# Self products over type-sorted nodes, a pass without branches, and one comparison for six row one-hots in a graph kernel

## The reference

```python
h = relu(layernorm(x))
xr = einsum('nd,rde->rne', h, W_rel)                       # 3 products
agg = segment_sum(xr[edge_type, src] + b_rel[edge_type], dst)
xs = einsum('nd,tde->tne', h, W_self)                      # 3 products
h_self = xs[node_type, arange(N)] + b_self[node_type]      # each node keeps one of them
x = x + relu(h_self + agg)
# layer 1: q, k, v from relu(layernorm(x)); softmax over the in-edges of each node; output product
```

## Time and profile before

| | us |
|---|---|
| runs of the kernel, median (lowest to highest) | 350.64 (350.07 to 350.78) |
| the profiled execution, its own time | 351.21 |
| its span, from the first to the last instruction | 349.4 |

### The profile page before, as it was taken

How to read it: one execution, slowest core, us unless ns; L and a number is a source line. 1 busy time by engine, 2 the same in 40 slices (tenths; PEclk the granted TensorE clock), 3 DMA queues, 4 the chain that set the end, 5 groups by cost and what they waited for, 6 DMA issues and landing times.

```text
span 349.4 us, 5835 instructions
## 1 busy us (share of the span) xinstructions
PE 310.5 (89%) x2113; PEld 247.3 (71%) x2113; DVE 213.7 (61%) x546; ACT 143.0 (41%) x276; POOL 70.0 (20%) x92
## 2 busy tenths in 40 slices
PE   3527449998999999999989999999899999999994
PEld 2104326766777777886878878999788888888883
DVE  5685994789994333343343695387685647574721
ACT  1009311151311333225234254367786655564621
POOL 4002350063250320337000141041000101010101
PEclk9999686999999999999999999999999999999999
DMA  5702311003021030000361000000000000000000
GB/s 166 240 1 60 123 63 58 2 1 120 3 83 40 3 122 2 2 3 2 120 190 52 1 0 2 0 2 0 1 3 2 2 30 2 32 2 32 2 32 27
DMA packets 7324, 14.19 MB, mean 41 GB/s; under 512 B 630, under 2 KB 646, under 8 KB 7290
## 3 DMA queue, kind: packets, MB, share of 16 engines
q1 hardware_dynamic: 6836, 13.13, 11.1%
q10 hardware_dynamic: 454, 0.61, 0.6%
HBM read 12.46 MB, written 1.28 MB: 39 GB/s over the span
## 4 chain that ended last, share of the span: by engine, by line
PE 74%; DVE 14%; ACT 4%; issue 3%; DMA 2%; DVEq 1%; POOL 0%; ACTq 0%
PE banks L1135 23%; PE banks L1081 8%; PE banks L1121 8%; PE banks L1215 7%; PE banks L1201 6%; PE banks L1190 6%; PE banks L1235 4%; PE banks L990 4%; DVE key_hot L725 3%; DVE row_hot L724 3%; DMA raw<-in_L_gnn_W_qkv_dram 2%; PE banks L1225 1%; PE banks L1111 1%; PE banks L1098 1%; PE banks L1067 1%
## 5 line engine op out<-in xcount | busy, mean ns | idle before, releaser
L389 POOL TENSOR_TENSOR w_hl<-raw,w_hl 128x512 fp32r<-128x512 f32 x24 | 30.6, 1298 | 88.4 <-ACT w_hl L457 88.4
L1135 PE MATMUL banks<-w_hl,hT 128*128 128x512 f32 x180 | 48.0, 418 | 0.0
L913 DVE CUSTOM_DVE_ANT_0 s_sb<-banks,mask_add 128x640 f32<-128x640 f32 x40 | 32.6, 821 | 22.1 <-PE banks L1190 22.0
L725 DVE TENSOR_SCALAR key_hot<-iota,picked 128x480 f16<-128x480 f16 x100 | 41.6, 416 | 0.0
L1135 PEld LDWEIGHTS banks<-w_hl,hT 128*128 128x128 f32 x180 | 35.2, 202 | 8.5 <-issue 0.2
L990 PE MATMUL banks<-key_hot,row_hot 128*128 128x480 f16 x100 | 28.4, 421 | 14.2 <-DVEq L755 14.0
L596 ACT ACTIVATE p_sb<-s_sb,neg_max 128x640 f32<-128x640 f32 x40 | 32.9, 823 | 17.3 <-DVE neg_max L913 17.3
L724 DVE TENSOR_SCALAR row_hot<-iota,picked 128x128 f16<-128x128 f16 x100 | 33.0, 330 | 6.5 <-issue 4.8
L1081 PE MATMUL banks<-adjT,h 128*128 128x320 f16 x240 | 33.8, 299 | 0.4 <-DVE zT_even L790 0.4
L466 ACT ACTIVATE adjT<-banks 128x480 f16<-128x480 f32 x20 | 11.3, 566 | 53.0 <-PE banks L1013 53.0
L1081 PEld LDWEIGHTS banks<-adjT,h 128*128 128x128 f16 x240 | 23.0, 98 | 10.5 <-issue 1.0
(11 more groups left out here) (160 smaller groups left out, 481.2 us busy)
## 6 DMA issues: line engine op xcount, KB each, us to landing
raw<-in_L_gnn_W_self_dram SPq DMA_DIRECT2D x3, 1024.0 KB, 5.8
raw<-in_L_gnn_W_rel_dram SPq DMA_DIRECT2D x3, 1024.0 KB, 5.2
raw<-in_L_gnn_W_qkv_dram SPq DMA_DIRECT2D x3, 1024.0 KB, 5.3
xs<-in_x_dram SPq DMA_DIRECT2D x1, 1024.0 KB
raw<-in_L_gnn_W_ff_dram SPq DMA_DIRECT2D x1, 1024.0 KB, 5.5
out_dram<-ybuf SPq DMA_DIRECT2D x4, 256.0 KB, 2.0
bv_rows<-in_L_gnn_b_qkv_dram ACTq DMA_DIRECT2D x1, 256.0 KB
bff_rows<-in_L_gnn_b_ff_dram ACTq DMA_DIRECT2D x1, 256.0 KB
```

Source lines behind the costliest of these rows:

```text
L389: nc.gpsimd.tensor_tensor(w_hl[q % 2][:, 1, kt], raw[q % 2][:, kt], w_hl[q % 2][:, 0, kt].bitcast(F32), ALU.subtract).then_inc(s_wlo, 1)
L725: return nc.vector.tensor_scalar(to_key, iota[:], float(KEYS * w), key, ALU.add, ALU.is_equal)
L913: nc.vector.tensor_tensor_reduce(s_sb[:, n % NS, :].rearrange("p (a j) -> p a j", a=2), banks[:, c:c + 2, 0:HALF], mask_add[:, it, :].rear ...
L1135: ins = mm(to, lhs[:, pl, kt, it * P:(it + 1) * P], weights[:, pw, kt, c0:c0 + cn], start=(start and n == 0), stop=(n == 3 * KD - 1), skip ...
```

## The change

1. **Self products over sorted nodes.** After the layer norm, the rows of `h` go to DRAM in the order of their type (each type starts at a multiple of 128), by five indirect scatters that POOL issues, one per tile, into a buffer that ACT's queue has first filled with zeros (1.8 MB). SP reads it back as 7 tiles (`hs`). PE transposes each tile (4 transposes) and multiplies it with its own type's weights only, as plain 32-bit floats: 4 matmuls of 512 columns, with the weights' place taken from a register. ACT copies both results out of PSUM. SP writes the 7 products to DRAM, and POOL gathers them back with five indirect transfers to `self_sum`. The 15 `self` units, the `hT` units, the split of `W_self` and the masking on DVE go. The positions come from ranks: one matmul with a triangle and five with ones on PE, and seven small chained instructions on DVE (`sorted_places`).
2. **No branches in the pass.** `G` is 6, so the loop for further chunks, the remainder and their register loads leave the windows. If a window had more than 6 chunks, all windows of the half would be counted again (`all_groups`, `all_chunks`), behind one branch for each half.
3. **One comparison for six row one-hots.** `row_hot` for a window is one `tensor_tensor` of two 16-bit tensors with 768 outputs a partition, one of them read with a step of 0 in the innermost dimension; the key one-hots stay as they are.
4. **Order.** The statistics come before window 1 on DVE. The pieces of the self products are `pipe`: two transposes and a product after window 6, then mostly one transpose and one product after each of windows 7 to 12. The relation weights 0 and 1 are split after the last of them.

```diff
-    G, F = 5, 3
+    G, F = 6, 1
+    PIPE_AT, PIPE_STEP = 6, 1
+    SORTED = NT + T - 1
...
-        side[2] = [("hT", 0, 0), ("hT", 1, 0)]
-        for it in range(2, NT):
-            side[it + 1].append(("hT", it, 0))
-        for n in range(T * NT):
-            side[5 + n].append(("self", n // NT, n % NT))
...
+        pipe = [("turn", 0), ("turn", 1)]
+        for t in range(SORTED):
+            pipe += [("self", t)] + [("turn", t + 2)] * (t + 2 < SORTED)
+        for n, u in enumerate(pipe):
+            pipe_side[PIPE_AT + max(n - 1, 0) * PIPE_STEP // 2].append(u)
...
+            self_weights(0)
+            sp.wait_ge(s_scat, 16 * NT)
+            for half, (t0, t1) in enumerate(((0, 2), (2, SORTED))):
+                sp.dma_start(hs[:, t0:t1, :], sorted_d[t0 * P:t1 * P, :].rearrange("(t p) d -> p t d", p=P)
+                             ).then_inc(s_hs[half], 16)
+            self_weights(1)
+            self_weights(2)
+            for q in range(R + 4):
+                if q == 2:
+                    for t in range(SORTED):
+                        sp.wait_ge(s_pcopy, pipe_no[("self", t)] + 1)
+                        sp.dma_start(self_d[t * P:(t + 1) * P, :], hs[:, t, :]).then_inc(s_kept, 16)
...
+            pool.wait_ge(s_place, 1)
+            pool.wait_ge(s_zero, 16)
+            for it in range(NT):
+                pool.wait_ge(s_y0, it + 1)
+                nc.gpsimd.indirect_dma_start(sorted_d, bass.IndirectOffsetOnAxis(ap=place_u[:, it:it + 1], axis=0),
+                                             in0[:, it, :], None).then_inc(s_scat, 16)
+            for it in range(NT):
+                pool.wait_ge(s_h16hi, it + 1)
+                nc.gpsimd.tensor_tensor(h16[:, 1, it, :], in0[:, it, :], h16[:, 0, it, :], ALU.subtract
+                                        ).then_inc(s_h16lo, 1)
             for kt in range(KD):
-                weights_lo(4, kt)
+                weights_lo(0, kt)
+            pool.wait_ge(s_kept, 16 * SORTED)
+            for it in range(NT):
+                nc.gpsimd.indirect_dma_start(self_sum[:, it, :], None, self_d,
+                                             bass.IndirectOffsetOnAxis(ap=place_u[:, it:it + 1], axis=0)
+                                             ).then_inc(s_self, 16)
+            for kt in range(KD):
+                weights_lo(1, kt)
...
+                nc.vector.tensor_tensor(row_hot[:, par], iota[:, 0:P].unsqueeze(1).broadcast_to([P, G, P]),
+                                        picked_row[:, w * G:(w + 1) * G].unsqueeze(2).broadcast_to([P, G, P]),
+                                        ALU.is_equal)
                 for k in range(G):
                     n = w * G + k
-                    one_hots(row_hot[:, par, k, :], key_hot[:, par, k, :], picked[:, 0, n:n + 1],
-                             picked[:, 1, n:n + 1], w).then_inc(s_hot, 1)
+                    key_one_hot(key_hot[:, par, k, :], picked[:, 1, n:n + 1], w).then_inc(s_hot, 1)
...
+            def pipe_unit(u):
+                kind, t = u
+                n = pipe_no[u]
+                if n >= 3:
+                    pe.wait_ge(s_pcopy, n - 2)
+                if kind == "turn":
+                    pe.wait_ge(s_hs[0 if t < 2 else 1], 16)
+                    for kt in range(KD):
+                        ins = nc.tensor.transpose(pipe_bank(u)[:, kt * P:(kt + 1) * P], hs[:, t, kt * P:(kt + 1) * P],
+                                                  ident[:])
+                else:
+                    pe.wait_ge(s_wself[min(t, T - 1)], 16)
+                    pe.wait_ge(s_pcopy, pipe_no[("turn", t)] + 1)
+                    for kt in range(KD):
+                        ins = mm(pipe_bank(u), hsT[:, t % 4, kt, :], w_self[:, bass.ds(offsets[t] + kt * D, D)],
+                                 start=(kt == 0), stop=(kt == KD - 1))
+                ins.then_inc(s_pipe, 1)
...
             def weights_hi(q):
                 act.wait_ge(s_raw[q % 2], 16 * (q // 2 + 1))
+                if q < 2:
+                    act.wait_ge(s_pipe, len(pipe))
```

More of the change, by code:

```diff
@@ L30 @@
 F8 = mybir.dt.float8e4
+U32 = mybir.dt.uint32
 I32 = mybir.dt.int32
@@ L187, in gnn_kernel @@
         s_taken = sem("s_taken")
-        s_win = sem("s_win")
+        s_again = sem("s_again")
+        s_copied = sem("s_copied")
+        s_stored = sem("s_stored")
+        s_half = sem("s_half")
         s_adj = sem("s_adj")
-        s_res = sem("s_res")
+        s_type = sem("s_type")
+        s_place = sem("s_place")
+        s_wself = [sem(f"s_wself{t}") for t in range(T)]
+        s_zero = sem("s_zero")
+        s_scat = sem("s_scat")
+        s_hs = [sem("s_hs0"), sem("s_hs1")]
+        s_pipe = sem("s_pipe")
+        s_pcopy = sem("s_pcopy")
+        s_kept = sem("s_kept")
+        s_self = sem("s_self")
         s_var = sem("s_var")
@@ L415, in _ @@
             for kt in range(KD):
-                weights_lo(5, kt)
+                weights_lo(2, kt)
             for it in range(NT):
@@ L848, in _ @@
             dve.wait_ge(s_fill, 11)
+            chain(nc.vector.tensor_scalar(picked_row[:], picked[:, 0, :], 1.0, None, ALU.add))
+            node_types()
             hot_group(0)
+            type_masks()
+            dve.wait_ge(s_x, 48)
+            for it in range(NT):
+                ins = nc.vector.bn_stats(stats[:, it, :], xs[:, it, :])
+            chain(ins)
+            for it in range(NT):
+                ins = nc.vector.bn_aggr(mv[:, 0, it, :], stats[:, it, :])
+            ins.then_inc(s_var, 1)
+            dve.wait_ge(s_fill, FILLS)
+            sorted_places()
+            dve.wait_ge(s_std, 1)
+            factors(0, 0, NT)
+            hot_group(1)
+            tile_types()
             window_bounds()
-            hot_group(1)
             chunk_keys()
-            dve.wait_ge(s_keys, EDGE_KEYS)
-            lo = load_bounds(dve, nc, bounds, 0, NW, EC)
-            hi = load_bounds(dve, nc, bounds, 1, NW, EC)
-            widest = dve.value_load(bounds[0:1, 2, NW:NW + 1], min_val=1, max_val=EC)
             asked = dve.alloc_register(name="asked_dve")
@@ L993, in _ @@
             first_chunks(0)
[L994 to L1014 removed]
+            pe.wait_ge(s_type, 1 + T)
@@ new lines, in _ @@
+            pe.wait_ge(s_fill, FILLS)
+            mm(banks[:, 4, 420:420 + NT * T], below[:], type_mask[:].rearrange("p n t -> p (n t)"), start=True,
+               stop=True, skip_group_check=True)
+            for it in range(NT):
+                ins = mm(banks[:, 4, 420 + (it + 1) * T:420 + (NT + 1) * T].rearrange("p (n t) -> p n t", t=T), ones[:],
+                         type_mask[:, it:it + 1, :].broadcast_to([P, NT - it, T]),
+                         start=False, stop=True, skip_group_check=True)
@@ new lines, in _, with all_chunks @@
+            ins.then_inc(s_prep, 1)
+            def all_chunks(half):
+                with pe.If(widest > G):
+                    pe.wait_ge(s_adj, stored[half])
+                    for w in range(half * NW // 2, (half + 1) * NW // 2):
+                        count = pe.value_load(bounds[0:1, 2, w:w + 1], min_val=1, max_val=EC)
+                        if w >= 2:
+                            pe.wait_ge(s_stored, w - 1)
+                        mm(banks[:, w % 2, 500:501], ident16[:], ident16[:, 0:1], start=True, stop=True,
+                           skip_group_check=True)
+                        with pe.Fori(0, count, F):
+                            pe.wait_ge(s_further, pe.snap(filled, min_val=1, max_val=1 << 20))
+                            pe.reg_add(filled, filled, F)
+                            for k in range(F):
+                                mm(banks[:, w % 2, 0:KEYS], further_row[:, k, :], further_key[:, k, :],
+                                   start=False, stop=True, skip_group_check=True).then_inc(s_taken, 1)
+                        mm(banks[:, w % 2, 500:501], ident16[:], ident16[:, 0:1], start=False, stop=True,
+                           skip_group_check=True).then_inc(s_again, 1)
```

326 lines of the change are left out of this document (176 added, 150 removed).

## The result

The changed kernel takes 334.91 us (median of 4 runs, 334.31 to 336.14), the kernel before 350.71 us (4 runs beside it, 350.07 to 351.2). The ratio is 0.9555, with a 95% interval of 0.9523 to 0.9587: faster by 15.8 us. The profiled execution took 335.22 us, its span is 333.5 us.

What follows compares the result with a forecast made beforehand. DVE was to bound the kernel until window 6, PE windows 6 to 12, DVE windows 13 to 19. The second `cnt` moves from 118.5 to 100.2, 18.3 us less: 351.2 to 332.9, as median 332.3 us; range 322 to 343.

Steps and rivals of the forecast that it cites:

- first part ends: From the start until window 6 is built, set by DVE: over at 39.7 us.
- third part: Windows 13 to 19 up to the second `cnt`, set by DVE: second `cnt` at 100.2 us.
- from the second `cnt` on: The program behind the second `cnt` unit, not changed: PE's 231 us left as they are.
- rival (a): In DVE's 12 groups on the path, the joint comparison takes two elements a cycle: 4.9 us less, 327.4; 12%.
- rival (b): Self tile at 1.7 us, 12 us less (320.3), or POOL's work missing DVE in windows 13 to 19, 7 us (325.3); 10% together.
- The 1.0 us for the clock: At PE's first transposes and self tile after window 6: 1.0 us added for the low clock after a wait.
- the one-hot of 1.3 us beside each piece: Sign for windows 13 to 19: a DVE one-hot of 1.3 us stands beside each of POOL's pieces.
- Rival (e): In windows 13 to 19 PE's clock falls to the lower level: +7 us, 339; 7%.
- the sign of being wrong: At the scatters and gathers: POOL's indirect transfers take over 3 us each.
- the slack of 8 us: Before PE's first transpose: sorted rows read back by 31.5 us, wanted at 39.7, so the transfers are hidden.
- rival (c): Slow scatters make PE wait before the first transpose, from 3.1 us each; at 4.5 each +7.3, 339.6; 14%.
- Rival (d): PE's wait before the first transpose eats the gain from 6.8 us a scatter; at 8 us each 357; 5%.

Runs made afterwards that it cites:

- the kernel with POOL late: The changed kernel with POOL waiting until DVE passed the second half's branch before splitting relation weight 0, gathering and splitting weight 1: 327.9 us (0.936).
- the wall alone gone: The changed kernel with only POOL's second four low parts (weight 1) waiting for the end of the pass: 333.79 us (0.9514).
- both gone: The changed kernel with POOL's second four low parts after the pass, plus 20 needless PE products after windows 14 and 15: 330.95 us (0.9475).

## Why the prediction was right, and where it was off

The forecast was 332.3 us, the time is 334.91: 2.6 us more, inside the range of 322 to 343. Its steps, in us:

| step | forecast | measured |
|---|---|---|
| a group of one-hots | 2.41 | 2.39 |
| the joint comparison, pitch | 0.88 | 0.87 |
| six chunks on PE | 1.24 | 1.22 |
| a self tile | 3.45 | 3.43 |
| first part ends | 39.7 | 38.84 |
| two transposes, first tile | 5.4 | 6.98 |
| windows 7 to 12 | 30.5 | 30.26 |
| third part | 24.6 | 26.97 |
| from the second `cnt` on | 230.9 | 230.4 |

**What held.** Which engine sets which part, in this order: DVE, PE, DVE; the last holds only as long as POOL's work stands there, as the kernel with POOL late shows. The price of the joint comparison was taken at the slower of two rates, 1.05 ns an element, and rival (a) is gone: 768 elements at a pitch of 0.87 us. The rule of the Trainium skill that stood beside it (Vector Engine (DVE) Microarchitecture Reference, section 5.1) agrees with this trace: 0.87 us, not 0.47. The self tile was bounded by 1.7 and 3.45, and the nearest row was right (3.43), which ends the first half of rival (b). POOL's other half of (b), that its work might miss DVE, is what a later order then brought (327.9 us; 325.3 was its price).

**The first tile.** The 1.0 us for the clock named the first product after a wait, 5.13 instead of 2.85 us; but that row says 2.3 us, not 1.0. (It is the second of the fifteen products, not the first, which stands at 42.29 us.) From 39 to 45 us the granted clock was 0.61 in the mean, and the transposes (1.91 us) as well as the first tile (5.10) were slow. The term was too small by 1.6 us; with the row's own 2.3 it would have been right to 0.3. The first part gave 0.9 us back: DVE was done with window 6's keys at 38.2 instead of 39.2.

**The third part** is the step that failed, by 2.4 us. It added up DVE's row: five groups, `cnt`, a `z` part, and 7 us for POOL. (Its terms give 100.1 us, not 100.2; nothing hangs on it.) The 7 us were right as a sum: 4.05 us in the group beside the first four pieces, 2.94 in the comparison beside the second four, 0.4 beside the gathers. But the one-hot of 1.3 us beside each piece, which was to show it, stands only beside the first four. What it left out is that DVE isn't always ready: it waited 2.20 us at 91.41 for the first `cnt` of PE, which came late (2.19 us for the half) and ran at the lower clock (4.21 us). Rival (e) had this cost, for the windows, with 7% and 7 us; it is there, but in one place and smaller. The experiments add what no sum of prices would have shown: with the first `cnt` over 2 us earlier, the third part is no shorter, as the second four pieces of POOL hold the comparison to 96.2 us all the same. With the wall alone gone it is 0.9 us shorter, with both gone 3.3 us.

**The transfers** were the weakest step. The five scatters were to begin at 19, take 1.3 us each and have landed at 28. They began at 20.21, though their positions were there at 16.9 (`place_u`): they also wait for the zeros, which were issued at 8.45 and landed 10.9 us later, at 19.4. They took 11.8 us (0.96 to 5.20 each, 2.1 in the mean, with 0.3 between them); the sign of being wrong, over 3 us each, was met by one of the five. SP's read back was issued at 33.82,

```profile
33.82 0.90 SPq L374 DMA_DIRECT2D hs<-sorted_rows  x2
```

and its first part, 512 KB, landed 3.8 us later, at 37.6. Of the slack of 8 us there were 1.2 left before PE's 38.84. So rival (c) was near: 1.2 us over five scatters is about 0.25 us more for each, and PE would have waited. The Trainium skill's rule (SBUF — State Buffer, "A bandwidth-pool intuition that's wrong") says that descriptors of GpSimd are locked out while DVE uses two ports. The rows agree in part: 2.22 and 5.20 us beside one-hots against 0.96 to 1.17 beside a still DVE. But in three kernels none was above 1.4 us beside one-hots, so the rule sets no fixed price here. Rival (d), slower than before, needed 6.8 us for each of the five; one single scatter in these runs took as much (7.07), and never two of a kernel.

## What to carry to other kernels

Where DVE and POOL share the path, don't add POOL's pieces to DVE's row as prices: mark where POOL's series ends, for here a one-hot could be held until that end, and what was saved ahead of it was lost there. Changes that gave 0.0 and 0.9 us apart gave 3.3 us together, so one that shows nothing alone isn't done with. Look what releases such a series (here ACT's splits, right after the last product) and move its start behind the stretch in which DVE feeds PE; spreading PE's long pieces over more windows did the same here at no cost seen. Compare traces from a point behind which they differ, not from their start: the first transpose moved by up to 2.1 us from trace to trace. When a transfer's slack rests on a duration that the trace doesn't have, keep its upper end in mind for the slack as well: here 8 us were in truth 1.2.

## What the hardware showed that was not expected

- A DVE one-hot can be held until a whole series of POOL's pieces of 1.2 to 1.3 us is over, not only until the next one: the joint comparison took 3.89, 5.84 and 6.36 us instead of 0.94, a single row one-hot 3.47, and at 27.54 us 3.98, instead of 0.25. The longest is in the kernel with only the second four late, beside POOL's five low parts of the features; it was done at 38.23 us, again 0.83 behind their end:

```profile
31.33 6.90 DVE L841 TENSOR_TENSOR row_hot<-iota,picked_row 128x768 f16<-128x768 f16 x1
```

```profile
31.82 5.58 POOL L458 TENSOR_TENSOR h<-in,h 128x512 f16<-128x512 f32 x5
```

- In other places POOL and DVE take turns, and each of POOL's pieces holds one one-hot: the six of 78.37 took 5.66 us beside four pieces. In the kernel with single comparisons a row one-hot takes 1.33 us while the key one-hot behind it takes 0.33. As single one-hots were held in both ways, it takes no second tensor as input to be held to the end; what decides was not found.

```profile
79.68 1.33 DVE L829 TENSOR_SCALAR row_hot<-iota,picked 128x128 f16<-128x128 f16 x1
80.93 0.33 DVE L833 TENSOR_SCALAR key_hot<-iota,picked 128x480 f16<-128x480 f16 x1
```

- An indirect transfer of 128 rows of 2 KB keeps POOL for 0.95 to 1.25 us where nothing holds it, with 0.30 us to the next; beside DVE's groups one took up to 7.07 us in one order, while in two others none took more than 1.24.
- 20 needless products changed nothing at one place and shortened the third part by 2.4 us at the same place once another wait was gone: that an experiment shows no gain doesn't show that its cause has no price.
